# Score maxima in five rounds in place of six, with two more PSUM banks, in a gated cross-attention block

## The chip, the cores and the metric

One core of one Trainium2 chip runs the whole kernel. The metric is the device time in microseconds (us) of one execution. A core has five engines with instruction streams of their own: PE (TensorE, the matrix unit, whose weight loads are shown apart as PEld), DVE (VectorE), ACT (ScalarE), POOL (GpSimd) and SP (SyncE, which here issues all DMAs). They meet at semaphores alone. PSUM, where PE writes its results, has eight banks of 128 partitions x 512 fp32 numbers.

## The reference, cut to what matters

Four sequences of 2048 tokens of width 512 are attended, with 16 heads of width 32, to 154 context tokens each; a feed-forward part with a token shift follows. Both are gated and added to their input.

```
x = x + tanh(g_xattn) * xattn(layernorm(x), ctx, Wq, Wk, Wv, Wo)
x = x + tanh(g_ffn)   * ffn(layernorm(x), W_r, W_k, W_v, mu_r, mu_k)

xattn:  Q = q Wq^T, K = c Wk^T, V = c Wv^T            (16 heads of 32)
        out = softmax(Q K^T / sqrt(32)) V Wo^T
ffn:    xr, xk = mu * x + (1 - mu) * (x of the token before)
        out = sigmoid(xr W_r^T) * (square(relu(xk W_k^T)) W_v^T)
```

The change touches one step of the softmax alone: the largest score of each token and head, which is subtracted before the exponential. The values that are computed stay the same.

## The kernel before

**Tiling.** The 8192 tokens are cut into 16 blocks of 512. A block has four token tiles of 128 (t = 0 to 3), and the 16 heads are four groups (g = 0 to 3) of four heads (j = 0 to 3), where head j of a group lies on partitions 32j to 32j+31 (`rows(j)`). Each big product is made of high and low parts of its operands: 12 matmuls of 128x128 by 512 columns (`product`, L1075; `ffn_k` writes its own out, L1240).

**Software pipeline.** `step(i)` of each engine handles the attention of block i together with the feed-forward part of block i-1 and the queries of block i+1. Steps 1 to 14 are a hardware loop; step 0 computes the keys and values of the context in place of the feed-forward part, and step 15 has no next block. The order on every engine is written out by hand; nothing is planned at run time. A wait holds everything behind it on its engine.

**Banks.** `s_bank0` to `s_bank3` take scores, `o_bank` and `d_bank` take the attention's values and its denominators (and later transposed tiles and mixed inputs of the feed-forward part), `g_bank0` and `g_bank1` take the big products in turn.

**Score maxima.** For each of the 16 pairs (g, t), four matmuls, one for each head j, give 128 tokens x 154 scores (L1137); their weights and their moving rows lie on the 32 partitions of head j. Head j always writes `s_bank[j]`, where three pairs fit side by side. The pairs come in six *rounds* (`ROUNDS`, L183): rounds 0 to 2 are t = 0 to 2 of group r, round 3 is t = 3 of groups 0 to 2, round 4 is t = 0 to 2 of group 3, and round 5 is the pair (3, 3). After each round DVE takes four maxima with `reduce_max` (L854), one for each bank, over 462 columns (154 in round 5). PE starts a round when `reduced` says that DVE is through with the round before. When all are there, `maxima_transposed` (L1148) turns the maxima on PE into `o_bank`, ACT copies them to `mT`, and the scores of the exponential are made with them.

**Where the rounds lie in PE's order** (L1352 to L1374, then L1288 to L1295). In the second half of step i: `query(i+1, 0)`; `query(i+1, 1)` with round 0 ahead of its third chunk of three matmuls; `query(i+1, 2)` with round 1 ahead of its fourth; `project(i, 0)` (the attention's output product of token tile 0) with round 2 ahead of its fourth; `project(i, 1)`; `project(i, 2)` with round 3 ahead of its first; `x2_transposed(i, 0)` (the normalised tile, transposed); `project(i, 3)`; `x2_transposed(i, 1)`; `query(i+1, 3)` with `x2_transposed(i, 2)` in it; `x2_transposed(i, 3)`; `ffn_v(i-1, 3)`; round 4. Then in step i+1: `ffn_k(i, (0, 1))`; round 5; `ffn_k(i, (2,))`, two chunks, `maxima_transposed(i+1)`, two chunks.

**Who waits beside it.** `project(i, t)` for t of 2 and 3 waits for `residual` t-2 on DVE (`x1_ready`, L1206), because both use one g bank. `x2_transposed(i, 0)` waits for the chain residual 0 (L890), moments (L819 to L824) on DVE, three small operations on POOL (L441 to L447), and the normalisation on ACT (L600). DVE's own order in that stretch is (L1023 to L1050): `attend(i, 3)`, the maxima of rounds 0, 1 and 2, residual 0, two maxima of round 3, residual 1, the other two maxima of round 3, residuals 2 and 3, the last normalisation (L898), then the mixing of the feed-forward inputs (L908, L921, L788), which PE's `ffn_k` needs. In step i+1 it goes on with the maxima of round 4, `mix_r(i, 0)` (L931), and the maxima of round 5.

Of the kernel before, what the change touches and what calls it, by code (L numbers as in the profile page):

```python
# [13 lines left out]
HI, LO = 0, 1  # L14
# [3 lines left out]
def flamingo_block(nc, x, ctx_columns, g_xattn, g_ffn, Wq, Wk, Wv, Wo, W_r, W_k, W_v, mu_r, mu_k, out):  # L18
# [10 lines left out]
    G = H // 4  # L29
    N = 512  # L30
    TT = N // P
    BLOCKS = B * T // N
    PER_BATCH = T // N
    S = 154
    TAIL = 32
# [13 lines left out]
    with ExitStack() as ctx:  # L49
# [28 lines left out]
        buf4 = sb("buf4", [P, 2, C, N], F32R)  # L78
# [76 lines left out]
        max_done = sem("max_done")  # L155
# [26 lines left out]

        ROUNDS = [[(g, t) for t in range(3)] for g in range(3)] + [[(g, 3) for g in range(3)], [(3, t) for t in range(3)], [(3, 3)]]  # L183
        MAX_UNITS = 4 * len(ROUNDS)
        xT_bank = [d_bank, s_bank[1], s_bank[2], s_bank[3]]
# [33 lines left out]
        LATER_STORES = [16 * (B - 1) if kind == "k" else 16 for _, kind, _ in KV[G + 2:]]  # L219
        kv_bank = s_bank[0:3] + s_bank[0:1] + [o_bank, d_bank] + [g_bank[n % 2] for n in range(7)]  # L220

# [25 lines left out]
        def later(eng, semaphore, value):  # L247

            if not isinstance(value, int) or value > 0:
                eng.wait_ge(semaphore, value)  # L250
# [535 lines left out]
        def _(dve):  # L786
# [56 lines left out]

            def reduce_max(i, r, heads=range(4)):

                (g, t), pairs = ROUNDS[r][0], len(ROUNDS[r])
                for j in heads:
                    if r == j == 0:
                        later(dve, mT_done, i)
                    dve.wait_ge(max_done, i * MAX_UNITS + 4 * r + j + 1)  # L850
                    scores = s_bank[j][:, 0:S * pairs].rearrange("p (n s) -> p n s", n=pairs)
                    column = TAIL * j + g
                    maxima = mm[:, t:t + pairs, column] if ROUNDS[r][-1][1] > t else mm[:, t, column:column + pairs]
                    nc.vector.reduce_max(maxima, scores, AX.X).then_inc(reduced, 1)  # L854
# [97 lines left out]
            dve.wait_ge(small_loaded, 64)  # L952
            for r in range(4):
                reduce_max(0, r)
                if r < 3:
                    weight_low(range(2 * C + 2 * r, 2 * C + 2 * r + 2))
# [8 lines left out]
            def step(i, ffn, pre):  # L965
                reduce_max(i, 4)
                if ffn:
                    mix_r(i - 1, 0)
                else:
                    kv_low_part(G + 1)  # L970
                reduce_max(i, 5)
                if not ffn:
# [55 lines left out]
                residual(i, 0, pre)  # L1028
                if pre:
                    reduce_max(i + 1, 3, (0, 1))  # L1030
                residual(i, 1, pre)
                if pre:
                    reduce_max(i + 1, 3, (2, 3))
                residual(i, 2, pre)
# [39 lines left out]
        def _(pe):  # L1074
# [14 lines left out]
            def cols(n):  # L1089
                return slice(P * n, P * n + P)  # L1090

            def rows(j):
                return slice(DH * j, DH * j + DH)

            def keys_or_values(u):

                item, kind, n = KV[u]
                if u == 0:
                    pe.wait_ge(ctx_lo, TILES[0])
                elif u == 3:  # L1100
                    pe.wait_ge(kv_lo, 1)
                elif u == G:
                    pe.wait_ge(w_lo, 3 * C)
                elif u == FIRST_LATER:
                    pe.wait_ge(ctx_lo, TILES[0] + TILES[1])
                    pe.wait_ge(q_copied, G)
                elif u > FIRST_LATER + 1:
                    pe.wait_ge(kv_lo, u - 1)
                if kind == "k":
                    product(kv_product(u), lambda s, c: buf1[:, s, c, cols(n)], lambda m, c: ctx_parts[item][:, m, c, 0:P * TILES[item]], C,  # L1110
                            (lambda c: pe.wait_ge(w_lo, c + 1)) if u == 0 else None).then_inc(kv_done, 1)
                else:
                    product(kv_product(u), lambda s, c: ctx_parts[item][:, s, c, cols(n)], lambda m, c: buf2[:, m, c, :], C).then_inc(kv_done, 1)
# [12 lines left out]
            def maxima(i, r):  # L1126

                if r == 0:
                    pe.wait_ge(k_loaded, 16 * K_LOADS * (i + 1))
                    later(pe, p_lo, i * SCORE_UNITS)  # L1130
                    pe.wait_ge(xT_lo, (i + 1) * TT)
                else:
                    pe.wait_ge(reduced, i * MAX_UNITS + 4 * r)
                pe.wait_ge(q_hi, i * G + ROUNDS[r][-1][0] + 1)
                for n, (g, t) in enumerate(ROUNDS[r]):
                    for j in range(4):
                        ins = nc.tensor.matmul(s_bank[j][:, S * n:S * n + S], buf4[rows(j), HI, g, cols(t)], k_all[rows(j), g, :],  # L1137
                                               start=True, stop=True)
                        if n == len(ROUNDS[r]) - 1:
                            ins.then_inc(max_done, 1)  # L1140

# [72 lines left out]

            def x2_transposed(i, t):
                if t < TT - 1:
                    pe.wait_ge(xn2_ready, i * (TT - 1) + t + 1)
                else:
                    pe.wait_ge(xn2_last, i + 1)
                if t < 2:  # L1220
                    pe.wait_ge(attn32_ready, (i + 1) * G)
                else:
                    pe.wait_ge(x2_ready, i * TT + t - 1)
                transposed(x2_bank[t], [xn2[t % 2][:, cols(c)] for c in range(C)]).then_inc(x2_done, 1)
# [45 lines left out]
            def at(chunk, what):  # L1270
                return lambda c: what() if c == chunk else None
# [9 lines left out]
            query(0, 2, False, at(1, lambda: maxima(0, 1)))  # L1281
            query(0, 3, False, at(1, lambda: maxima(0, 2)))
            maxima(0, 3)
            keys_or_values(G)
            maxima(0, 4)

            def step(i, ffn, pre):
                if ffn:  # L1288
                    ffn_k(i - 1, (0, 1))
                    maxima(i, 5)  # L1290
                    ffn_k(i - 1, (2,), before=at(2, lambda: maxima_transposed(i)))
                else:
                    keys_or_values(G + 1)
                    maxima(i, 5)
                    maxima_transposed(i)  # L1295
# [56 lines left out]
                if pre:  # L1352
# [10 lines left out]
                    project(i, 1, pre)  # L1363
                    project(i, 2, pre, at(0, lambda: maxima(i + 1, 3)))
                    x2_transposed(i, 0)
# [6 lines left out]
                    if ffn:  # L1372
                        ffn_v(i - 1, 3)
                    maxima(i + 1, 4)  # L1374
                else:
                    ffn_r(i - 1, 3)
                    for t in range(3):
                        project(i, t, pre)
                    x2_transposed(i, 0)
                    project(i, 3, pre)  # L1380
                    x2_transposed(i, 1)
                    v_product(i - 1, 3, V3_END, lambda c: x2_transposed(i, c) if c >= 2 else None)

# [46 lines left out]
```

## Time and profile before

| | us |
|---|---|
| runs of the kernel before | 1411.4 median, 1409.05 to 1411.85 (3 runs) |
| the profiled execution's own time | 1411.68 |
| its span, first to last instruction | 1409.9 |
| PE busy | 1357.0 (96%) |
| DVE busy | 1043.5 (74%) |
| ACT busy | 777.4 (55%) |
| POOL busy | 574.7 (41%) |

The span is the time between the first and the last instruction; 1.8 us lie around it. A busy share is an average over stages, and matmuls are pipelined, so that a busy PE is not PE at its peak: small gaps between matmuls of different shape hide in it. The granted clock of PE was 0.989 of full speed over the span, and 1.00 in the steady blocks. In the timeline a row gives the start, the time from the first start to the last end, the engine, the line, the tiles and shapes, the number of instructions, and in brackets the idle time of the engine before it with what ended it.

### The profile page before, as it was taken

The numbers are of one execution on the slowest core, as the hardware profiler recorded it, in microseconds if no ns is written. First come the engines' busy times: TensorE is split into PE (matmuls) and PEld (weight loads), VectorE is DVE, ScalarE is ACT, GpSimd is POOL, SyncE is SP. The second block draws the span as 40 slices with busy tenths as digits, with TensorE's granted clock in tenths as the row PEclk, the third lists the DMA queues.
The fourth block names the chain that finished last, engine by engine and source line by source line (L and its number), as shares of the span: only waits on it lengthen the run. The fifth ranks groups of instructions, "written<-read, shape, count | busy, mean of one in ns | idle before, by whom it ended". The sixth has DMA issues, their size and how long they took to land.

```text
span 1409.9 us, 27976 instructions
## 1 busy us (share of the span) xinstructions
PE 1357.0 (96%) x9436; PEld 991.6 (70%) x9436; DVE 1043.5 (74%) x1940; ACT 777.4 (55%) x1440; POOL 574.7 (41%) x774
## 2 busy tenths in 40 slices
PE   4979999999999999999999999999999999999988
PEld 4657677776767777676777767677776767767667
DVE  4787868687786867778686876868777686877662
ACT  3583746647374663736456374655637465563632
POOL 2113535344352534435353353525344353444433
PEclk7999999999999999999999999999999999999999
DMA  6630121211112121111212011121202112110101
GB/s 187 218 93 18 53 61 52 74 51 42 33 60 67 52 73 37 46 44 60 67 52 66 24 66 44 60 67 52 60 22 74 44 52 74 52 57 17 46 23 46
DMA packets 98795, 84.07 MB, mean 60 GB/s; under 512 B 49488, under 2 KB 63824, under 8 KB 98768
## 3 DMA queue, kind: packets, MB, share of 16 engines
q1 hardware_dynamic: 98768, 83.72, 19.5%
q8 instruction: 15, 0.25, 0.1%
q14 instruction: 12, 0.10, 0.0%
HBM read 58.79 MB, written 20.71 MB: 56 GB/s over the span
## 4 chain that ended last, share of the span: by engine, by line
PE 79%; DVE 9%; ACT 8%; issue 3%; POOL 0%; DMA 0%; ACTq 0%; DVEq 0%
PE g_bank L1080 45%; PE g_bank L1240 7%; PE o_bank L1187 6%; PE s_bank L1161 4%; PE d_bank L1193 4%; ACT s_bank L641 3%; ACT pq L640 3%; PE s_bank L1137 3%; PE s_bank L1171 2%; DVE buf L788 2%; PE d_bank L1086 2%; DVE o_bank L921 2%; PE o_bank L1086 1%; DVE d_bank L921 1%; ACT buf L546 1%
## 5 line engine op out<-in xcount | busy, mean ns | idle before, releaser
L858 DVE TENSOR_TENSOR pq<-s_bank,pq 128x512 f16<-128x512 f32 x320 | 220.2, 689 | 70.2 <-ACT s_bank L641 70.0
L854 DVE TENSOR_REDUCE mm<-s_bank 128x3 f32<-128x462 f32 (+1 forms) x384 | 199.0, 579 | 93.2 <-PE s_bank L1137 93.0
L640 ACT ACTIVATE pq<-s_bank 128x512 f16<-128x512 f32 x320 | 192.3, 601 | 87.2 <-PE s_bank L1165 87.2
L1080 PE MATMUL g_bank<-xnT,WqT 128*128 128x512 f32 x768 | 200.0, 407 | 4.4 <-DVE xnT L842 4.4
L1240 PE MATMUL g_bank<-buf,WkT 128*128 128x512 f32 x744 | 195.8, 410 | 8.6 <-DVE buf L788 6.5
L641 ACT ACTIVATE s_bank<-s_bank 128x512 f32<-128x512 f32 x320 | 194.6, 608 | 0.0
L1080 PE MATMUL g_bank<-WoT,buf 128*128 128x512 f32 x768 | 193.3, 401 | 0.0
L1080 PE MATMUL g_bank<-WrT,buf 128*128 128x512 f32 x744 | 183.5, 395 | 0.0
L477 POOL TENSOR_TENSOR buf<-place,buf 128x512 fp32r<-128x512 f32 x64 | 82.5, 1290 | 235.9 <-ACT buf L546 235.9
L1080 PE MATMUL g_bank<-WvT,buf 128*128 128x512 f32 x708 | 174.2, 395 | 0.0
L1240 PEld LDWEIGHTS g_bank<-buf,WkT 128*128 128x128 f32 x744 | 136.0, 191 | 51.4 <-DVE buf L788 13.8
L1080 PEld LDWEIGHTS g_bank<-xnT,WqT 128*128 128x128 f32 x768 | 140.3, 191 | 40.7 <-DVE xnT L842 5.9
L1080 PEld LDWEIGHTS g_bank<-WrT,buf 128*128 128x128 f32 x744 | 137.3, 188 | 39.6 <-issue 10.9
L1080 PEld LDWEIGHTS g_bank<-WoT,buf 128*128 128x128 f32 x768 | 140.7, 188 | 32.7
L1080 PEld LDWEIGHTS g_bank<-WvT,buf 128*128 128x128 f32 x708 | 130.6, 188 | 32.6 <-issue 5.8
L465 POOL TENSOR_TENSOR buf<-xa,buf 128x512 fp32r<-128x512 f32 x64 | 82.1, 1283 | 161.9 <-DVE d_bank L921 82.0
L546 ACT ACTIVATE buf<-place 128x512 fp32r<-128x512 f32 x128 | 81.1, 633 | 107.0 <-DVE place L875 72.5
L473 POOL TENSOR_TENSOR buf<-place,buf 128x512 fp32r<-128x512 f32 x64 | 83.3, 1301 | 93.8 <-ACT buf L546 93.8
L485 POOL TENSOR_TENSOR x<-place,x 128x512 f32<-128x512 f32 x48 | 61.7, 1284 | 123.1 <-DVE place L885 123.1
L600 ACT ACTIVATE xa<-x,nb,rstd 128x512 f32<-128x512 f32 x48 | 39.0, 813 | 105.1 <-POOL nb L447 104.9
L469 POOL TENSOR_TENSOR place<-place 128x512 f32<-128x512 f32 x64 | 78.2, 1222 | 24.4 <-ACT place L632 24.4
L869 DVE STREAM_TRANSPOSE place<-d_bank 128x512 f32<-128x512 f32 x64 | 45.4, 709 | 55.5 <-PE d_bank L1193 55.5
(142 smaller groups left out, 2071.8 us busy)
## 6 DMA issues: line engine op xcount, KB each, us to landing
xa<-in_x SPq DMA_DIRECT2D x64, 256.0 KB, 3.4
x<-in_x SPq DMA_DIRECT2D x64, 256.0 KB, 2.7
out<-x SPq DMA_DIRECT2D x48, 256.0 KB, 2.0
k_all<-k_scratch SPq DMA_DIRECT2D x16, 256.0 KB, 2.8
k_low<-k_scratch SPq DMA_DIRECT2D x16, 256.0 KB, 3.0
v_main<-v_scratch SPq DMA_DIRECT2D x16, 256.0 KB, 2.8
place<-x SPq DMA_DIRECT2D x16, 256.0 KB, 2.4
out<-place SPq DMA_DIRECT2D x16, 256.0 KB, 2.0
```

The lines of the kernel that those rows point to most:

```text
L465: nc.gpsimd.tensor_tensor(buf4[:, LO, g, :], q32[g], buf4[:, HI, g, :].bitcast(F32), ALU.subtract).then_inc(q_lo, 1)
L469: nc.gpsimd.tensor_tensor(k2[c % 2], k2[c % 2], k2[c % 2], ALU.mult).then_inc(k2_ready, 1)
L473: nc.gpsimd.tensor_tensor(buf1[:, LO, c, :], k2[c % 2], buf1[:, HI, c, :].bitcast(F32), ALU.subtract).then_inc(k2_lo, 1)
L477: nc.gpsimd.tensor_tensor(buf3[:, LO, g, :], attn32, buf3[:, HI, g, :].bitcast(F32), ALU.subtract).then_inc(attn_lo, 1)
L546: nc.scalar.activation(dst, src, ACT.Copy).then_inc(done, 1)
L640: nc.scalar.activation(pq[:, n, HI, :], bank[:, :], ACT.Exp, scale=SCALE).then_inc(p_hi, 1)
L641: nc.scalar.activation(bank[:, :], bank[:, :], ACT.Exp, scale=SCALE).then_inc(p_full, 1)
L854: nc.vector.reduce_max(maxima, scores, AX.X).then_inc(reduced, 1)
L858: nc.vector.tensor_tensor(pq[:, n, LO, :], score_bank[5 * g + n][:, :], pq[:, n, HI, :], ALU.subtract).then_inc(p_lo, 1)
L1080: ins = nc.tensor.matmul(dst, stationary(s, c), moving(m, c), start=(c, n) == (0, 0), stop=(c, n) == (chunks - 1, len(PRODUCTS) - 1))
L1187: nc.tensor.matmul(o_bank[rows(j), :], v, pq[:, 4 if n else j, q, :], start=(n, k) == (0, 0), stop=(n, k) == (1, 2))
L1240: ins = nc.tensor.matmul(bank[c][:, :], WkT2[:, s, e, cols(c)], buf3[:, m, e, :], start=(e, n) == (0, 0), stop=(e, n) == (C - 1, len(PRODU ...
```

## The change

The rounds become lists of *units*: a unit is a bank, a head and the pairs (g, t) whose scores stand side by side in that bank, and one maximum on DVE. There are five rounds. Rounds 0 to 2 keep t = 0 to 2 of group r for all four heads in the s banks, and have two units more in `o_bank` and `d_bank`: in round 0 the pair (0, 3) of heads 0 and 1; in round 1 the pairs (0, 3) and (1, 3) of heads 2 and 3; in round 2 the pairs (1, 3) and (2, 3) of heads 0 and 1. The new round 3 is the former round 4. The new round 4 (the last) has the pair (3, 3) of heads 0 and 1, and (2, 3) and (3, 3) of heads 2 and 3. The 64 matmuls of a block are in rounds of 14, 16, 16, 12 and 6; the maxima are 6, 6, 6, 4 and 4 (26 where there were 24), over 154 columns four times, 308 six times and 462 sixteen times. Within a round the matmuls go pair by pair, and in each through the units in the order o, d, s0, s1, s2, s3.

The round ahead of `project(i, 2)` goes, and on DVE the two halves of its maxima between the residuals. Round 0 also waits for the attention of the block (`attn32_ready`), and `x2_transposed` of tiles 0 and 1 waits for all maxima of rounds 0 to 2 where it waited for the attention. In block 0 the context's value product `keys_or_values(G)` is placed ahead of the new round 3, and it and all later context products use the g banks, with waits for the queries' copies in place of the o and d banks.

```diff
@@ -180,8 +180,21 @@
-        ROUNDS = [[(g, t) for t in range(3)] for g in range(3)] + [[(g, 3) for g in range(3)], [(3, t) for t in range(3)], [(3, 3)]]
-        MAX_UNITS = 4 * len(ROUNDS)
+        def unit(bank, head, *pairs):
+            return bank, head, pairs
+        def alone(g):
+            return [unit(s_bank[j], j, *((g, t) for t in range(3))) for j in range(4)]
+        ROUNDS = [
+            [unit(o_bank, 0, (0, 3)), unit(d_bank, 1, (0, 3))] + alone(0),
+            [unit(o_bank, 2, (0, 3), (1, 3)), unit(d_bank, 3, (0, 3), (1, 3))] + alone(1),
+            [unit(o_bank, 0, (1, 3), (2, 3)), unit(d_bank, 1, (1, 3), (2, 3))] + alone(2),
+            alone(3),
+            [unit(s_bank[j], j, (3, 3)) for j in range(2)] + [unit(s_bank[j], j, (2, 3), (3, 3)) for j in (2, 3)]]
+        FIRST_UNIT = [sum(len(units) for units in ROUNDS[:r]) for r in range(len(ROUNDS) + 1)]
+        MAX_UNITS = FIRST_UNIT[-1]
         xT_bank = [d_bank, s_bank[1], s_bank[2], s_bank[3]]
@@ -217,7 +230,7 @@
         LATER_STORES = [16 * (B - 1) if kind == "k" else 16 for _, kind, _ in KV[G + 2:]]
-        kv_bank = s_bank[0:3] + s_bank[0:1] + [o_bank, d_bank] + [g_bank[n % 2] for n in range(7)]
+        kv_bank = s_bank[0:3] + s_bank[0:1] + [g_bank[(n + 1) % 2] for n in range(9)]
@@ -841,16 +854,15 @@
-            def reduce_max(i, r, heads=range(4)):
-
-                (g, t), pairs = ROUNDS[r][0], len(ROUNDS[r])
-                for j in heads:
-                    if r == j == 0:
+            def reduce_max(i, r):
+                for n, (bank, j, pairs) in enumerate(ROUNDS[r]):
+                    if r == n == 0:
                         later(dve, mT_done, i)
-                    dve.wait_ge(max_done, i * MAX_UNITS + 4 * r + j + 1)
-                    scores = s_bank[j][:, 0:S * pairs].rearrange("p (n s) -> p n s", n=pairs)
-                    column = TAIL * j + g
-                    maxima = mm[:, t:t + pairs, column] if ROUNDS[r][-1][1] > t else mm[:, t, column:column + pairs]
+                    dve.wait_ge(max_done, i * MAX_UNITS + FIRST_UNIT[r] + n + 1)
+                    (g, t), column = pairs[0], TAIL * j + pairs[0][0]
+                    scores = bank[:, 0:S * len(pairs)].rearrange("p (n s) -> p n s", n=len(pairs))
+                    maxima = mm[:, t, column:column + len(pairs)] if t == TT - 1 else mm[:, t:t + len(pairs), column]
                     nc.vector.reduce_max(maxima, scores, AX.X).then_inc(reduced, 1)
@@ -950,7 +962,7 @@
             dve.wait_ge(small_loaded, 64)
-            for r in range(4):
+            for r in range(3):
                 reduce_max(0, r)
@@ -963,12 +975,12 @@
             def step(i, ffn, pre):
+                reduce_max(i, 3)
+                if ffn:
+                    mix_r(i - 1, 0)
+                else:
+                    kv_low_part(G + 1)
                 reduce_max(i, 4)
-                if ffn:
-                    mix_r(i - 1, 0)
-                else:
-                    kv_low_part(G + 1)
-                reduce_max(i, 5)
                 if not ffn:
@@ -1026,11 +1038,7 @@
                 residual(i, 0, pre)
-                if pre:
-                    reduce_max(i + 1, 3, (0, 1))
                 residual(i, 1, pre)
-                if pre:
-                    reduce_max(i + 1, 3, (2, 3))
                 residual(i, 2, pre)
@@ -1095,6 +1103,8 @@
                 item, kind, n = KV[u]
+                if u in (G, G + 1):
+                    pe.wait_ge(q_copied, u - 1)
                 if u == 0:
@@ -1103,8 +1113,7 @@
                     pe.wait_ge(ctx_lo, TILES[0] + TILES[1])
-                    pe.wait_ge(q_copied, G)
-                elif u > FIRST_LATER + 1:
+                if u >= FIRST_LATER:
                     pe.wait_ge(kv_lo, u - 1)
@@ -1128,16 +1137,19 @@
                     later(pe, p_lo, i * SCORE_UNITS)
+                    later(pe, attn32_ready, i * G)
                     pe.wait_ge(xT_lo, (i + 1) * TT)
                 else:
-                    pe.wait_ge(reduced, i * MAX_UNITS + 4 * r)
-                pe.wait_ge(q_hi, i * G + ROUNDS[r][-1][0] + 1)
-                for n, (g, t) in enumerate(ROUNDS[r]):
-                    for j in range(4):
-                        ins = nc.tensor.matmul(s_bank[j][:, S * n:S * n + S], buf4[rows(j), HI, g, cols(t)], k_all[rows(j), g, :],
-                                               start=True, stop=True)
-                        if n == len(ROUNDS[r]) - 1:
-                            ins.then_inc(max_done, 1)
+                    pe.wait_ge(reduced, i * MAX_UNITS + FIRST_UNIT[r])
+                pe.wait_ge(q_hi, i * G + min(r, G - 1) + 1)
+                for n in range(3):
+                    for bank, j, pairs in ROUNDS[r]:
+                        if n < len(pairs):
+                            g, t = pairs[n]
+                            ins = nc.tensor.matmul(bank[:, S * n:S * n + S], buf4[rows(j), HI, g, cols(t)], k_all[rows(j), g, :],
+                                                   start=True, stop=True)
+                            if n == len(pairs) - 1:
+                                ins.then_inc(max_done, 1)
@@ -1212,15 +1224,17 @@
-            def x2_transposed(i, t):
+            def x2_transposed(i, t, pre=True):
                 if t < TT - 1:
                     pe.wait_ge(xn2_last, i + 1)
-                if t < 2:
+                if t >= 2:
+                    pe.wait_ge(x2_ready, i * TT + t - 1)
+                elif pre:
+                    pe.wait_ge(reduced, (i + 1) * MAX_UNITS + FIRST_UNIT[3])
+                else:
                     pe.wait_ge(attn32_ready, (i + 1) * G)
-                else:
-                    pe.wait_ge(x2_ready, i * TT + t - 1)
                 transposed(x2_bank[t], [xn2[t % 2][:, cols(c)] for c in range(C)]).then_inc(x2_done, 1)
@@ -1280,18 +1294,17 @@
             query(0, 3, False, at(1, lambda: maxima(0, 2)))
+            keys_or_values(G)
             maxima(0, 3)
-            keys_or_values(G)
-            maxima(0, 4)
                     ffn_k(i - 1, (0, 1))
-                    maxima(i, 5)
+                    maxima(i, 4)
                     ffn_k(i - 1, (2,), before=at(2, lambda: maxima_transposed(i)))
                     keys_or_values(G + 1)
-                    maxima(i, 5)
+                    maxima(i, 4)
                     maxima_transposed(i)
@@ -1361,7 +1374,7 @@
                     project(i, 1, pre)
-                    project(i, 2, pre, at(0, lambda: maxima(i + 1, 3)))
+                    project(i, 2, pre)
                     x2_transposed(i, 0)
@@ -1371,15 +1384,15 @@
                         ffn_v(i - 1, 3)
-                    maxima(i + 1, 4)
+                    maxima(i + 1, 3)
                 else:
                         project(i, t, pre)
-                    x2_transposed(i, 0)
+                    x2_transposed(i, 0, pre)
                     project(i, 3, pre)
-                    x2_transposed(i, 1)
-                    v_product(i - 1, 3, V3_END, lambda c: x2_transposed(i, c) if c >= 2 else None)
+                    x2_transposed(i, 1, pre)
+                    v_product(i - 1, 3, V3_END, lambda c: x2_transposed(i, c, pre) if c >= 2 else None)
```

## Rows read from the trace of the kernel before

**Rows 1.** The page's chain of work that ended last, by engine.

```profile
PE 79%; DVE 9%; ACT 8%; issue 3%; POOL 0%; DMA 0%; ACTq 0%; DVEq 0%
```

**Rows 2.** Windows: length, busy time of each engine (instructions), clock, DMA share, GB/s.

```profile
608.68:691.62 82.94, 82.14 (x582) 59.84 (x581) 63.40 (x118) 46.99 (x87) 35.63 (x48) 1.00 0.18 54
```

**Rows 3.** Critical chain of one block, in order: start, length, what.

```profile
630.96 0.62 PE d_bank L1086 x4
...
638.17 3.05 PE g_bank L1240 x12
```

**Rows 4.** Timeline, PE: round 3 and the product behind it.

```profile
620.51 0.57 PE L1137 MATMUL s_bank<-k_all,buf 32*128 32x154 f32 x12
621.01 3.06 PE L1080 MATMUL g_bank<-WoT,buf 128*128 128x512 f32 x12
```

**Rows 5.** Timeline, PE, single matmuls about round 3 and project(i, 2).

```profile
620.19 0.40 PE L1080 MATMUL g_bank<-WoT,buf 128*128 128x512 f32 x1
...
621.36 0.39 PE L1080 MATMUL g_bank<-WoT,buf 128*128 128x512 f32 x1
...
623.68 0.39 PE L1080 MATMUL g_bank<-WoT,buf 128*128 128x512 f32 x1
...
624.58 0.40 PE L1080 MATMUL g_bank<-WoT,buf 128*128 128x512 f32 x1
```

**Rows 6.** The same about round 5 and, last, behind `maxima_transposed`.

```profile
640.83 0.39 PE L1240 MATMUL g_bank<-buf,WkT 128*128 128x512 f32 x1
...
641.15 0.34 PE L1137 MATMUL s_bank<-k_all,buf 32*128 32x154 f32 x4
...
641.76 0.39 PE L1240 MATMUL g_bank<-buf,WkT 128*128 128x512 f32 x1
...
643.60 0.39 PE L1240 MATMUL g_bank<-buf,WkT 128*128 128x512 f32 x1
```

**Rows 7.** Three narrow stretches in round 2: matmuls running; the second holds two passes.

```profile
616.33 0.35 PE L1137 MATMUL s_bank<-k_all,buf 32*128 32x154 f32 x4
...
616.51 0.39 PE L1137 MATMUL s_bank<-k_all,buf 32*128 32x154 f32 x8
...
616.62 0.28 PE L1137 MATMUL s_bank<-k_all,buf 32*128 32x154 f32 x4
```

**Rows 8.** Timeline, DVE: maxima of rounds 1 and 2, residual 0.

```profile
613.43 2.28 DVE L854 TENSOR_REDUCE mm<-s_bank 128x3 f32<-128x462 f32 x4 [1.87 <-PE s_bank L1137]
...
616.92 2.28 DVE L854 TENSOR_REDUCE mm<-s_bank 128x3 f32<-128x462 f32 x4 [1.22 <-PE s_bank L1137]
619.12 0.68 DVE L890 TENSOR_TENSOR x<-g_bank,x 128x512 f32<-128x512 f32 x1
```

**Rows 9.** Timeline, DVE: maxima of round 5 and the next operation.

```profile
641.61 0.99 DVE L854 TENSOR_REDUCE mm<-s_bank 128x1 f32<-128x154 f32 x4
642.51 0.69 DVE L788 TENSOR_TENSOR buf<-d_bank,buf 128x512 fp32r<-128x512 f32 x1
```

**Rows 10.** Timeline: the normalisation of tile 0 on ACT, its transposes' weight loads on PE.

```profile
622.06 0.82 ACT L600 ACTIVATE xa<-x,nb,rstd 128x512 f32<-128x512 f32 x1 [6.64 <-POOL nb L447]
...
623.68 0.59 PEld L1086 LDWEIGHTS o_bank<-ident,xa 128*128 128x128 f32 x4
```

**Rows 11.** Timeline: `maxima_transposed`, weight loads on PE.

```profile
642.73 0.57 PEld L1086 LDWEIGHTS o_bank<-ident,mm 128*128 128x128 f32 x4
```

**Rows 12.** Timeline: DVE releases `x2_transposed(i, 3)`; the second matmul behind it.

```profile
630.30 0.55 DVE L898 TENSOR_SCALAR xa<-x,mv,rstd 128x512 f32<-128x512 f32 x1 [1.14 <-POOL rstd L443]
...
630.90 0.42 PEld L1086 LDWEIGHTS d_bank<-ident,xa 128*128 128x128 f32 x4 [0.38 <-DVE xa L898]
...
631.63 0.39 PE L1080 MATMUL g_bank<-WvT,buf 128*128 128x512 f32 x1
```

**Rows 13.** Timeline, block 0: the last maxima on DVE, their transposes on PE.

```profile
55.88 0.98 DVE L854 TENSOR_REDUCE mm<-s_bank 128x1 f32<-128x154 f32 x4
...
56.92 0.66 PE L1086 MATMUL o_bank<-ident,mm 128*128 128x128 f32 x4 [1.72 <-DVE mm L854]
```

More of the change, by code:

```diff
@@ L965, in step @@
             def step(i, ffn, pre):
-                reduce_max(i, 4)
+                reduce_max(i, 3)
                 if ffn:
@@ L970, in step @@
                     kv_low_part(G + 1)
-                reduce_max(i, 5)
+                reduce_max(i, 4)
                 if not ffn:
```

## The prediction

> **What bounds the kernel now.** I read the page's chain of waits first: PE is 79% of it, DVE 9%, ACT 8% [rows 1]. Then the windows: a steady block takes 82.94 us, in which PE is busy 82.14 us and DVE 63.40 [rows 2]. So PE has no room; whatever a round costs PE is paid in the block's time, as is whatever makes PE wait. But the chain leaves PE once in each block: from the end of `x2_transposed(i, 3)` at 631.58 (630.96 + 0.62) it runs over ACT and DVE and comes back to PE at 638.17 [rows 3]. That stretch hangs on `project(i, 3)` by residual 3, the last normalisation and the last transposes, so it starts later or earlier as `project(i, 3)` does, and PE's work beside it hides nothing. I therefore follow two things: when `project(i, 3)` runs, and when `maxima_transposed` runs. All behind each shifts with it.
>
> **What a round costs PE.** Round 3 has 12 matmuls; 0.50 us pass from its first to the next product's first [rows 4]. That is not all, since the weight loads are no longer ahead. From the last full matmul before it to the second behind it are 621.36 - 620.19 = 1.17 us; without the round two pitches would lie there, each (623.68 - 621.36) / 10 = 0.23 us [rows 5]. Cost: 0.71 us. For round 5 (4 matmuls) the same sum is 641.76 - 640.83 - 0.46 = 0.47 us [rows 6]. In round 2 the matmuls start in passes of four heads: 616.33, 616.51, 616.62 [rows 7]. So a further pass costs 0.11 us (0.12 by the difference of the two rounds), and a round has a fixed cost of about 0.36 us.
>
> Removing the round ahead of `project(i, 2)` gives back 0.71 us. Its scores come back elsewhere. What that costs depends on why four start together. If it is because they lie on different partitions, the passes of a round are as many as the matmuls of its commonest head. In the new round 0 heads 0 and 1 occur four times, in round 1 heads 2 and 3 five times, in round 2 heads 0 and 1 five times, in the last round heads 2 and 3 twice. That is 1, 2, 2 and 1 passes more: 0.11, 0.22, 0.22 and 0.11 us. If only the number of matmuls counts, they cost (0.71 - 0.47) / 8 = 0.03 us each: 0.06, 0.12, 0.12 and 0.06. From below zero is the bound (the matmuls hide between others); from above 0.18 us a pass, the longest distance in rows 7. I take the passes, since the trace shows starts in clusters with gaps between, not evenly. PE alone then gains 0.71 - 0.66 = 0.05 us a block: the change removes a fixed cost and pays nearly all of it in passes.
>
> The Trainium skill bears on this from two sides. "TensorE: Matmul & The Clock Gate", Part 3 (Packing small matmuls), says that a weight load overlaps running matmuls only where its row group is another one; by that, the repeated heads make passes. "TensorEngine Tiling (Array Packing)", Instruction Overhead, gives each matmul an overhead of about 60 cycles; by that the count matters, and the second sum holds. No row of before shows a head repeated out of turn.
>
> **What the maxima cost DVE.** Four maxima over 462 columns take 619.12 - 616.92 = 2.20 us, 0.55 each [rows 8]; over 154 columns 642.51 - 641.61 = 0.90 us, 0.225 each [rows 9]. Between them, 308 columns cost 0.39 us. Round 0 grows by 0.45 us, rounds 1 and 2 by 0.78 each, the last by 2 x 0.165 = 0.33; the two halves between the residuals (2.2 us) go. DVE idled 1.87 us before round 1's maxima and 1.22 us before round 2's [rows 8], so 0.45 and 0.78 are hidden. (Close: round 1's end now at 613.43 + 2.28 + 0.11 + 0.78 = 616.60, and PE wants round 2 at 616.33 + 0.33 = 616.66.) Round 2's 0.78 us are not hidden, for residual 0 stands right behind them.
>
> **First place: `x2_transposed(i, 0)`.** Residual 0 starts later by 0.33 us (passes of rounds 0 and 1) and 0.78: 619.12 + 1.11 = 620.23 us. In round 2 the first unit is complete at the third pass, as the first bank was before, so nothing is won there. Behind residual 0 come moments, POOL and ACT, all of which waited for their input: the normalisation ended at 622.06 + 0.82 = 622.88 us [rows 10], and ends now at 623.99. A release takes about 0.05 us (630.30 + 0.55 to 630.90 [rows 12]), so the transposes start at 624.04. PE wanted them at 623.68 [rows 10]; with 0.71 off and 0.55 on, at 623.52. (`project(i, 2)` itself needs residual 0: done at 620.91, released at 620.96, where PE could have begun its loads just before; 0.1 us, which drowns in the wait that follows.) So the slack of 0.75 us which these transposes had is overdrawn by 0.4 us. Behind released transposes the second matmul of the next product starts 631.63 - 630.90 = 0.73 us after [rows 12]: at 624.77, where it was at 624.58 [rows 5]. `project(i, 3)` is 0.19 us later, in place of 0.16 earlier. What was gained by residuals 1 and 2 being free of maxima helps nobody, as they wait for the projections or had time.
>
> **Second place: `maxima_transposed`.** DVE runs without a gap into the last round's maxima, so their end moves from 642.60 (641.61 + 0.99) to 642.93 [rows 9], release 642.98. PE wanted to load at 642.73 [rows 11], now 642.84 with the pass. The second matmul behind was at 643.60 [rows 6]; by the 0.73 it is now at 643.71, and if the 0.14 us of wait added to the pass in full, at 643.85. I take 0.13 us of loss. The new waits beside these cost nothing: for `attn32_ready` PE has 18 query matmuls, 4.2 us by the pitch, between the attention's last matmul and round 0, in which DVE needs four operations, each no longer than the 0.7 us of a 512-column one; and the maxima that `x2_transposed(i, 0)` waits for stand ahead of residual 0 on DVE. PE has queued behind `maxima_transposed` half of `ffn_k(2)` and the scores, for which ACT's exponentials wait, so the loss goes on.
>
> **Block 0.** The value product moved ahead of the round saves a stall, but kv_low_part and the later maxima wait for the same context product as before; I count nothing, with half a us to each side. The last maxima add their 0.33 us in full, since PE already waits 1.72 us for them [rows 13].
>
> **Sum.** `project(i, 3)` with a next block occurs in 15 blocks: 15 x 0.19 = 2.9 us. The last round outside block 0 occurs 15 times: 15 x 0.13 = 1.9. Block 0: 0.3. Together +5.1 us. The profiled execution took 1411.68 us (span 1409.9 and 1.8 around it), so 1416.8; the median of the runs is 0.3 us less: 1416.5 us.
>
> **The rivals.**
> *The count of matmuls decides.* Then residual 0 is 0.18 + 0.78 later, the second matmul of `project(i, 3)` is at 624.62, +0.04 us, and `maxima_transposed` costs 0.11, since there DVE decides. 15 x 0.15 + 0.3 = +2.6 us: 1414.0. If the added matmuls cost nothing at all, -0.14 and +0.11: 15 x -0.03 + 0.3 = -0.1 us, 1411.2. For it: four matmuls issue within hundredths. Against: the gaps of rows 7.
> *PE's saving is kept (the other side).* If the chain from round 2's maxima to `x2_transposed(i, 0)` is not what PE meets, as the slack of 0.75 us might be taken to mean, and the count decides, PE gains 0.71 - 0.30 = 0.41 us there and loses 0.06 to 0.11 in the last round: 15 x -0.33 + 0.3 = -4.7 us: 1406.7. It decides as soon as the normalisation of tile 0 ends before 623.2. Against it is plain adding: 0.78 us of maxima lie on that chain whatever PE does. A maximum over 308 columns would have to take under half of what I interpolate, or stand in DVE's idle time before the round ends.
> *A pass out of turn costs 0.18 us.* Residual 0 is then 0.54 + 0.78 later, `project(i, 3)` +0.40, the last round +0.20: 15 x 0.6 + 0.4 = +9.4 us: 1420.8.
>
> **How the numbers follow.** Forecast 0.50; count decides, or something near it, 0.27; dear passes 0.12; saving kept 0.11. This kernel's measurement can tell a change of 0.2%, 2.8 us, from none: 1408.6 to 1414.2. The forecast and the dear passes are slower (0.62), the count is within (0.27), the saving is faster (0.11). The range leaves out the saving and the worst of the dear passes: 1411.0 to 1420.0. The forecast's own range is 1414.5 to 1418.
>
> **What would show it.** Right: a steady block of 83.2 to 83.3 us; round 1 and 2 in five clusters of starts; residual 0 about 1.1 us later after round 2's start of before; in front of `x2_transposed(i, 0)` an idle PE weight path released by ACT L600, which rows 10 do not have; `maxima_transposed` released by DVE L854. Wrong: `x2_transposed(i, 0)` without a wait, or starts of repeated heads 0.03 us apart. A block under 82.7 us would refute the whole.

## The result, and the profile after

| | before | changed |
|---|---|---|
| median of the runs, us | 1411.74 (8 runs) | 1415.66 (8 runs) |
| ratio, 95% interval | | 1.0033 (1.0019 to 1.0046) |
| profiled execution, us (span) | 1411.68 (1409.9) | 1413.76 (1412.0) |
| a steady block, us | 82.94 [rows 2] | 83.34 |
| PE's granted clock over the span | 0.989 | 0.991 |

The change makes the kernel slower by 3.9 us at the median (0.28%; the ratio says 0.33%); the forecast was 1416.5 us and a block of 83.2 to 83.3. The two profiled executions differ by only 2.1 us, which misleads: the 14 blocks of the loop, cut at the same query matmul in both kernels, cost 5.7 us more (1167.74 - 1162.02), and what lies outside of them 3.6 less. A reader has to cut the span before comparing. Windows: length, busy time of each engine, clock, DMA share, GB/s; the changed kernel's start, its 14 blocks, one block, and last a stretch where its start differs.

```profile
0.00:103.05 103.05, 73.22 (x544) 54.77 (x545) 73.28 (x141) 61.98 (x116) 23.52 (x54) 0.90 0.54 169
103.05:1270.79 1167.74, 1152.83 (x8113) 837.60 (x8109) 888.85 (x1679) 656.37 (x1218) 496.73 (x657) 1.00 0.18 53
...
604.08:687.42 83.34, 82.45 (x585) 59.89 (x581) 63.52 (x120) 46.88 (x87) 35.61 (x47) 1.00 0.18 53
...
100.00:110.00 10.00, 9.72 (x85) 6.76 (x85) 7.06 (x14) 3.44 (x7) 2.52 (x2) 1.00 0.51 104
```

The same of the kernel before:

```profile
0.00:105.82 105.82, 76.95 (x544) 56.36 (x544) 72.16 (x139) 61.79 (x116) 22.80 (x54) 0.89 0.53 166
105.82:1267.84 1162.02, 1148.34 (x8112) 836.54 (x8108) 887.15 (x1651) 657.91 (x1218) 497.25 (x657) 1.00 0.18 53
...
100.00:110.00 10.00, 9.32 (x66) 5.46 (x66) 5.55 (x9) 4.17 (x9) 0.83 (x1) 0.83 0.41 85
```

And of a second execution of the changed kernel, under its own windows:

```profile
0.00:105.86 105.86, 76.96 (x544) 56.72 (x545) 73.11 (x141) 61.80 (x116) 23.52 (x54) 0.89 0.53 166
100.00:110.00 10.00, 9.27 (x66) 5.48 (x66) 5.55 (x9) 4.19 (x9) 0.79 (x1) 0.83 0.40 82
```

In one execution of the changed kernel the start took 103.05 us, in the other 105.86; a clock of 1.00 in one and 0.83 in the other between 100 and 110 us goes with it (these windows do not hold the same work, so the clock is a companion here, not a cause that was shown). So 2.8 us of the start come and go with one kernel, and are no part of the change. The steady blocks hardly vary: behind the first one they took 82.93 to 82.94 us before, 83.32 to 83.35 in the changed kernel, and 83.29 to 83.33 in its second execution, so differences under some 0.03 us between two kernels say nothing.

Within a block the changed kernel shows what was forecast. Timeline, round 2 to `project(i, 3)`; the block starts at 604.08, that of before at 604.36:

```profile
616.33 0.33 PE L1149 MATMUL o_bank<-k_all,buf 32*128 32x154 f32 x1
...
616.92 0.48 DVE L866 TENSOR_REDUCE mm<-o_bank 128x2 f32<-128x308 f32 x1 [0.65 <-PE s_bank L1149]
...
617.32 0.47 DVE L866 TENSOR_REDUCE mm<-d_bank 128x2 f32<-128x308 f32 x1
617.70 2.27 DVE L866 TENSOR_REDUCE mm<-s_bank 128x3 f32<-128x462 f32 x4
619.89 0.68 DVE L902 TENSOR_TENSOR x<-g_bank,x 128x512 f32<-128x512 f32 x1
...
620.62 2.62 PEld L1088 LDWEIGHTS g_bank<-WoT,buf 128*128 128x128 f32 x12 [0.25 <-DVE x L902]
...
622.84 0.81 ACT L613 ACTIVATE xa<-x,nb,rstd 128x512 f32<-128x512 f32 x1 [7.42 <-POOL nb L460]
...
623.77 0.42 PEld L1094 LDWEIGHTS o_bank<-ident,xa 128*128 128x128 f32 x4 [0.53 <-issue]
...
624.16 0.99 PEld L1088 LDWEIGHTS g_bank<-WoT,buf 128*128 128x128 f32 x5
```

Counted from the block's start, residual 0 begins at 15.81 us (before: 619.12 - 604.36 = 14.76), the normalisation of tile 0 ends at 19.57 (18.52), its transposes load at 19.69 (19.32 [rows 10]) behind an idle weight path of 0.53 us, and the next product's loads begin at 20.08 (624.24 - 604.36 = 19.88 before): 0.2 us late. The idle time is marked "issue", not ACT; that ACT is what PE waits for is read from the ACT row, which ends 0.12 us ahead, and put to the test by the second run below. At the second place:

```profile
641.09 0.46 PE L1149 MATMUL s_bank<-k_all,buf 32*128 32x154 f32 x6
641.48 1.65 PE L1254 MATMUL g_bank<-buf,WkT 128*128 128x512 f32 x6
641.53 1.31 DVE L866 TENSOR_REDUCE mm<-s_bank 128x1 f32<-128x154 f32 x4
642.97 0.42 PEld L1094 LDWEIGHTS o_bank<-ident,mm 128*128 128x128 f32 x4 [0.27 <-issue]
...
643.36 0.30 PEld L1254 LDWEIGHTS g_bank<-buf,WkT 128*128 128x128 f32 x2
```

The last round takes 0.39 us where it took 0.27, and the weight path, which showed no idle time before these transposes [rows 11], idles 0.27, again marked "issue". The waits of the whole trace, in which L1094 into `o_bank` stands for both places (total, times, longest), name ACT in two cases only:

```profile
PEld o_bank L1094 <- issue: 11.0, 28, 0.5
...
PEld o_bank L1094 <- ACT xa L613: 1.0, 2, 0.5
```

### The profile page after: what moved, and what is told of

Same layout as the page of the kernel before. It is cut to its first block, busy times and chain, and to the rows that moved or that the text cites. A ratio compares the mean times of both kernels' runs of the same rounds, so it can differ in the third digit from the quotient of the medians.

```text
span 1412.0 us, 27993 instructions
## 1 busy us (share of the span) xinstructions
PE 1356.7 (96%) x9436; PEld 989.8 (70%) x9436; DVE 1047.1 (74%) x1972; ACT 776.0 (55%) x1440; POOL 575.2 (41%) x774
## 4 chain that ended last, share of the span: by engine, by line
PE 79%; DVE 9%; ACT 8%; issue 3%; POOL 0%; DMA 0%; ACTq 0%; DVEq 0%
PE g_bank L1088 45%; PE g_bank L1254 7%; PE o_bank L1199 6%; PE s_bank L1173 4%; PE d_bank L1205 4%; ACT s_bank L654 3%; ACT pq L653 3%; PE s_bank L1183 2%; DVE buf L801 2%; PE o_bank L1094 2%; PE d_bank L1094 2%; PE s_bank L1149 2%; DVE o_bank L933 2%; DVE d_bank L933 1%; ACT buf L559 1%
## 5 line engine op out<-in xcount | busy, mean ns | idle before, releaser
L866 DVE TENSOR_REDUCE mm<-s_bank 128x3 f32<-128x462 f32 (+2 forms) x320 | 166.2, 583 | 1.3 <-PE s_bank L1149 1.3
L478 POOL TENSOR_TENSOR buf<-xa,buf 128x512 fp32r<-128x512 f32 x64 | 83.0, 1296 | 165.3 <-ACT xa L632 83.2
L486 POOL TENSOR_TENSOR buf<-place,buf 128x512 fp32r<-128x512 f32 x64 | 83.2, 1301 | 96.8 <-ACT buf L559 96.8
```

The source lines that it names most:

```text
L478: nc.gpsimd.tensor_tensor(buf4[:, LO, g, :], q32[g], buf4[:, HI, g, :].bitcast(F32), ALU.subtract).then_inc(q_lo, 1)
L486: nc.gpsimd.tensor_tensor(buf1[:, LO, c, :], k2[c % 2], buf1[:, HI, c, :].bitcast(F32), ALU.subtract).then_inc(k2_lo, 1)
```

## Experiments

All blocks below are windows of one steady block. Those with a ratio were run five rounds beside the kernel before; the others were executed once, and their times alone tell little.

**The changed kernel again.** No edit.

> The changed kernel unedited, as the base of the three beside it on the same chip. Theory (two waits: the transposes of tile 0 behind residual 0, and the transposed maxima behind the last round): a steady block of 83.34 us as in its first trace, where the kernel before has 82.94; 15 x 0.40 = 6 us, less what block 0 saves, so about 5 us (0.3 to 0.4%) slower than before. Rival (the difference is a clock effect of the start): a block of 83.34 us all the same, but a time within 0.2% of before.

```profile
608.08:691.37 83.29, 82.41 (x585) 59.91 (x581) 63.50 (x120) 46.86 (x87) 35.60 (x47) 1.00 0.18 53
```

1416.82 us against 1411.53, ratio 1.0041 (1.0025 to 1.0056). The slowdown is real.

**Round 2's o and d maxima behind residual 0.**

`reduce_max` takes the units to do as a third argument.

```diff
-                    reduce_max(i + 1, 2)
+                    reduce_max(i + 1, 2, range(2, 6))
                 residual(i, 0, pre)
+                if pre:
+                    reduce_max(i + 1, 2, (0, 1))
```

> The maxima over the o and d banks of round 2 are taken behind residual 0 and its moments, not ahead; nothing else is changed, and PE's order is the same. Theory: residual 0 comes 0.78 us earlier, the normalised tile 0 is there before PE wants it, the weight path has no idle time before the transposes of tile 0 that ACT ended, and project(i, 3) runs 0.19 us earlier than in the kernel before in place of 0.21 later. A steady block of 82.94 us, 0.40 less than the changed kernel, 15 x 0.40 = 6 us less in all. Rival (PE's added passes are the cost, the wait is incidental): the block stays at 83.3 us.

The block, and the first place (block start 603.45):

```profile
603.45:686.37 82.92, 82.11 (x584) 60.08 (x580) 63.51 (x120) 46.96 (x87) 35.62 (x47) 1.00 0.18 54
```

```profile
621.66 0.82 ACT L613 ACTIVATE xa<-x,nb,rstd 128x512 f32<-128x512 f32 x1 [6.87 <-POOL nb L460]
...
622.60 0.58 PEld L1098 LDWEIGHTS o_bank<-ident,xa 128*128 128x128 f32 x4
```

1411.35 us, ratio 1.0004 (0.9992 to 1.0017). The transposes load at 19.15 us of the block, 0.17 earlier than before and without a wait. One order on DVE is worth 0.4 us a block, as much as the whole loss. PE's order and its added passes were the same, so the rival falls. The block is that of before because two terms cancel: the 0.16 us that PE gains (0.71 less the passes of rounds 0 to 2) now show, and pay for the second place, whose loss is still there.

**The last round without its added pair.**

```diff
-            [unit(s_bank[j], j, (3, 3)) for j in range(2)] + [unit(s_bank[j], j, (2, 3), (3, 3)) for j in (2, 3)]]
+            [unit(s_bank[j], j, (3, 3)) for j in range(4)]]
```

> The pair (2, 3) of heads 2 and 3 is left out of the last round: its two matmuls and its columns in two maxima (four maxima over 154 columns remain, as in the kernel before), so those maxima are not computed. Theory: the transposed maxima are no longer late, 0.18 us less a block: 83.16 us, 2.7 us less in all. Rival (only PE's added pass counts there, DVE's 0.33 us are hidden): 0.11 us less, 83.23 us. Second rival (ACT's exponentials or DVE set the pace behind it and absorb the shift): no change, 83.34 us.

```profile
602.70:685.89 83.19, 82.30 (x582) 59.85 (x578) 63.18 (x120) 46.87 (x87) 35.66 (x47) 1.00 0.17 53
```

```profile
641.28 0.59 PEld L1094 LDWEIGHTS o_bank<-ident,mm 128*128 128x128 f32 x4
```

1412.2 us, ratio 1.0013 (1.0001 to 1.0024). The idle time of 0.27 us before the transposed maxima is gone, so it was DVE that PE waited for. But the block lies between the theory (83.16) and the pass alone (83.23) and does not tell them apart: it is 0.10 to 0.15 us under the two executions of the changed kernel, and the pass alone is 0.12. What the wait costs beside the pass is at most 0.06 us, and is not shown to be more than nothing. The second rival falls.

**Both at once.** The two edits above.

> The maxima over the o and d banks of round 2 behind residual 0, and the last round without the pair (2, 3) of heads 2 and 3 (its scores and maxima are left out). Theory (two losses that add, and under them PE's own saving): 83.34 - 0.40 - 0.16 = 82.78 us a block, 0.16 under the kernel before, some 2.4 us less than it in all, 0.17%. Rival (the two are one chain, of which one cure is enough): 82.94 us, as with the first cure alone.

```profile
602.25:685.05 82.80, 82.01 (x582) 60.03 (x578) 63.17 (x120) 46.98 (x87) 35.60 (x47) 1.00 0.18 54
```

1409.52 us against 1411.6, ratio 0.9985 (0.9976 to 0.9994). The two losses add (82.92 less 82.80 is 0.12, the pass again), so the rival of one chain falls. Rid of both, the five rounds are 0.14 us a block better than the six: what is left of the removed round's 0.71 us once the passes of rounds 0 to 2 are paid. But this kernel leaves one pair's maxima of two heads out, so it is no version to keep.

**The o and d matmuls of a round first.**

```diff
-                for n in range(3):
-                    for bank, j, pairs in ROUNDS[r]:
+                spare = len(ROUNDS[r]) - 4
+                for n, units in [(n, ROUNDS[r][:spare]) for n in range(2)] + [(n, ROUNDS[r][spare:]) for n in range(3)]:
+                    for bank, j, pairs in units:
```

> In rounds 0 to 2 PE does all matmuls of the o and d banks ahead of those of the s banks; the passes of a round stay as many. Theory: in round 2 the first maximum can start one pass, 0.11 us, earlier, and the whole chain over residual 0 to the transposes of tile 0 with it: a block of 83.23 us. Rival (the chain is not what binds): 83.34 us. If the passes are not set by the commonest head but by order, rounds 1 and 2 change their length of 0.71 us from first matmul to the next product's first.

```profile
603.16:686.37 83.21, 82.37 (x585) 59.95 (x581) 63.49 (x120) 46.88 (x87) 35.65 (x47) 1.00 0.18 53
```

1415.79 us, ratio 1.0031 (1.0019 to 1.0042). The block lost 0.13 us, as one pass earlier should give; the ratio alone could not have told it from the changed kernel. Round 2 kept its length: 0.72 us from its first matmul to the next product's (615.40 to 616.12), so the order of the matmuls within a round does not set it.

**What sets a round's length.** On the kernel before, repeated matmuls in rounds 0 and 1.

```diff
+                again = {0: [0, 1, 2, 3], 1: [0, 0]}.get(r, [])
                 for n, (g, t) in enumerate(ROUNDS[r]):
-                    for j in range(4):
+                    for k, j in enumerate((again if n == 2 else []) + [0, 1, 2, 3]):
...
-                        if n == len(ROUNDS[r]) - 1:
+                        if n == len(ROUNDS[r]) - 1 and k >= (len(again) if n == 2 else 0):
```

> A probe of what sets a round's length on PE, on the kernel before: round 0 repeats one pair for all four heads (16 matmuls, the commonest head four times), round 1 repeats it for head 0 alone, twice (14 matmuls, the commonest head five times), round 2 is left at 12. The repeated scores overwrite equal ones. Measured is the distance from a round's first matmul to the next product's first, 0.50 us for 12 in the kernel before. Theory (passes, as many as the matmuls of the commonest head, 0.11 us each): 0.61 us for round 0 and 0.72 for round 1. Rival (0.03 us for each matmul): 0.62 for round 0 and 0.56 for round 1.

Timeline, PE: 16 matmuls balanced over the heads, then 14 with one head five times, each with the product behind it.

```profile
608.69 0.68 PE L1138 MATMUL s_bank<-k_all,buf 32*128 32x154 f32 x16
609.29 3.69 PE L1080 MATMUL g_bank<-xnT,WqT 128*128 128x512 f32 x15
612.92 0.78 PE L1138 MATMUL s_bank<-k_all,buf 32*128 32x154 f32 x14
613.63 0.74 PE L1080 MATMUL g_bank<-xnT,WqT 128*128 128x512 f32 x2
```

0.60 us for 16 and 0.71 for 14: fewer matmuls, longer round. The commonest head counts, not the number. The rule that a weight load overlaps only with matmuls of other row groups (the Trainium skill, "TensorE: Matmul & The Clock Gate", Part 3) agrees; the sum by an overhead of each matmul falls. The kernel took 1416.28 us, its block 83.27, 0.33 more than before for 0.31 us of added passes: nothing hides a pass on PE.

```profile
604.37:687.64 83.27, 82.49 (x591) 60.16 (x587) 63.38 (x118) 46.98 (x87) 35.64 (x47) 1.00 0.18 53
```

**The slack in the kernel before.** Two, and then three, added maxima ahead of residual 0.

```diff
+                    if r == 2 and j == 3:
+                        for extra in range(2):
+                            nc.vector.reduce_max(mm[:, 0:2, 8 + extra], s_bank[j][:, 0:2 * S].rearrange("p (n s) -> p n s", n=2), AX.X)
```

> The kernel before, with two maxima over 308 columns added on DVE in round 2, ahead of its last one, into columns that nothing uses: 0.78 us more in front of residual 0 (what the change adds there), with PE's work as it was. Theory (the transposes of tile 0 had 0.75 us of slack and the chain adds one to one): they are released at about the moment at which PE wants them, a block of 82.94 to 82.97 us. Rival (the chain had no slack, all of it is lost): 83.7 us.

> The same with three added maxima, 1.17 us. Theory: the slack of 0.75 us is overdrawn by 0.42, of which the transposes give back 0.15 since their loads and matmuls are then closer: project(i, 3) 0.25 us later, a block of 83.19 us, and an idle time of PE's weight path before these transposes that ACT ended. Rival (more slack than 0.75 us): 82.94 us.

The blocks were 83.25 and 83.66 us. Both expectations miss, by 0.3 and 0.5 us. The single times were 1414.46 and 1425.01 us, where the kernel before took 1413.73: the second fits its block (11.3 us for 15 x 0.72), the first does not (0.7 us for 15 x 0.31), which a single execution cannot settle. The blocks and rows of the first and, below, of the second:

```profile
603.90:687.15 83.25, 82.22 (x585) 59.86 (x581) 64.06 (x120) 46.99 (x87) 35.63 (x47) 1.00 0.18 53
```

```profile
619.43 0.68 DVE L893 TENSOR_TENSOR x<-g_bank,x 128x512 f32<-128x512 f32 x1
...
620.35 0.57 PE L1140 MATMUL s_bank<-k_all,buf 32*128 32x154 f32 x12 [0.23 <-DVE x L893]
...
623.52 0.59 PEld L1089 LDWEIGHTS o_bank<-ident,xa 128*128 128x128 f32 x4
```

```profile
609.87:693.53 83.66, 82.26 (x585) 59.85 (x581) 64.42 (x121) 46.99 (x87) 35.62 (x47) 1.00 0.19 53
```

```profile
626.70 0.56 PE L1140 MATMUL s_bank<-k_all,buf 32*128 32x154 f32 x12 [0.61 <-DVE x L893]
```

In the kernel before, round 3 stands inside `project(i, 2)`, behind its wait for residual 0 (`x1_ready`, L1206). That gate shuts first: 0.78 us more cost 0.31, and 1.17 cost 0.72, so it had about 0.46 us of slack, and the round's fixed cost comes after it. The transposes behind had 0.75, but it was never they that PE met here: they loaded 0.3 us later than before (623.52 - 603.90 = 19.62 us of the block) and without a wait of their own. This is read from the rows; no run took the gate away. The change takes round 3 away from this gate, so that there the transposes decide; the prediction had both waits for the changed kernel, but my expectations for these two runs had forgotten the first.

**Block 0 in the old order.**

```diff
+            maxima(0, 3)
             keys_or_values(G)
-            maxima(0, 3)
```

and on DVE the maxima of round 3 of block 0 ahead of `kv_low_part(G)`.

> The changed kernel with the old order in block 0 alone: round 3 ahead of the context's value product, and its maxima ahead of kv_low_part(G). Theory (that move is what hid the 0.33 us that the last round's maxima grew by in block 0): from the first matmul of round 0 to the first of the transposed maxima 19.85 us in place of the 19.52 of both kernels. Rival (the g banks or their waits did it, or nothing had to be hidden): 19.52 us.

Rounds 0 and 3 and the transposed maxima on PE, and between them DVE and POOL:

```profile
37.32 0.30 PE L1150 MATMUL o_bank<-k_all,buf 32*128 32x154 f32 x1
...
48.87 0.57 PE L1150 MATMUL s_bank<-k_all,buf 32*128 32x154 f32 x12 [0.95 <-DVE mm L866]
...
57.87 0.66 PE L1095 MATMUL o_bank<-ident,mm 128*128 128x128 f32 x4 [2.25 <-DVE mm L866]
```

```profile
48.73 2.43 DVE L810 SCALAR_TENSOR_TENSOR WoT<-WoT_loaded,gate,WoT 128x512 fp32r<-128x512 f32 x2
```

```profile
49.12 1.50 POOL L478 TENSOR_TENSOR buf<-xa,buf 128x512 fp32r<-128x512 f32 x1 [2.12 <-ACT xa L632]
```

20.55 us (57.87 - 37.32), where both kernels have 19.52: the move hid 1.03 us, three times what was expected. What I had left out are the bigger maxima of rounds 0 to 2. With round 3 ahead of the value product PE waits 0.95 us for them, where it had no wait in the kernel before, and the value product behind it, for which ACT and then DVE wait, starts 12.05 us behind round 0 (49.37 - 37.32) in place of 10.64 before (48.04 - 37.40). The changed kernel has the product ahead of that wait.

**A try for a faster version.** The first edit, and `mix_r(0)` on DVE behind the last round's maxima, on ACT `mT_copy` ahead of `xr_high(0)`.

```diff
-                    mix_r(i - 1, 0)
...
                 reduce_max(i, 4)
+                if ffn:
+                    mix_r(i - 1, 0)
```

> Full computation. The maxima over the o and d banks of round 2 behind residual 0, and on DVE mix_r(0) behind the maxima of the last round, on ACT the copy of the transposed maxima ahead of the high part of that mix. Theory: the wait for DVE in front of the transposed maxima goes, which is the smaller half of the second loss (0.06 us; the other 0.12 is PE's added pass and stays): 82.88 us a block against 82.94 with the first edit alone, 0.9 us less. Rival: the mixed input comes 1.2 us later, and the feed-forward product that needs it, ffn_r(0), or the exponentials behind its high part on ACT wait: a block above 82.94 us.

1465.06 us, ratio 1.0380 (1.0365 to 1.0395): the rival, far beyond what I had given it. Two blocks, and the timeline around the exponentials:

```profile
621.85:708.68 86.83, 83.80 (x585) 60.97 (x581) 65.17 (x120) 47.11 (x87) 35.22 (x47) 0.98 0.17 51
708.68:794.50 85.82, 82.39 (x585) 60.03 (x581) 65.16 (x120) 47.11 (x87) 35.20 (x47) 1.00 0.17 52
```

```profile
662.12 0.69 DVE L802 TENSOR_TENSOR buf<-d_bank,buf 128x512 fp32r<-128x512 f32 x1 [1.28 <-ACT buf L559]
...
662.68 1.28 POOL L486 TENSOR_TENSOR buf<-place,buf 128x512 fp32r<-128x512 f32 x1 [3.08 <-ACT buf L559]
662.85 1.68 DVE L946 SCALAR_TENSOR_TENSOR d_bank<-place,mu,x 128x512 f32<-128x512 f32 x1
663.92 1.49 POOL L482 TENSOR_TENSOR place<-place 128x512 f32<-128x512 f32 x1
664.44 1.53 DVE L946 SCALAR_TENSOR_TENSOR o_bank<-place,mu,x 128x512 f32<-128x512 f32 x1
...
669.21 1.65 PE L1188 MATMUL s_bank<-buf,k_tail 128*128 128x512 f32 x3 [2.73 <-DVE pq L873]
```

```profile
669.00:671.20 2.20, 1.99 (x5) 1.61 (x6) 2.00 (x4) 2.20 (x6) 1.52 (x2) 0.50 0.00 0
```

The wait at the transposed maxima did go. But three things were lost. The moved mix came later, and DVE then idled 1.28 us for its high part from ACT: the low part above starts at 40.27 us of the block, with the first edit alone at 38.29 (641.74 - 603.45), 2.0 us earlier. Then two mixes, 0.76 us each with the first edit alone, ran beside POOL's operations and took 1.68 and 1.53 us, 1.7 more. ACT's high parts, its exponentials and the tail scores followed; PE idled 2.73 us, and in this block it then ran with a clock of 0.50, the lower of its two levels (1.2 GHz). In the next block the clock stayed at 1.00, and it took 85.82 us: so 2.9 us of the loss are the late chain, and about 1.0 more, in the blocks where the clock fell, is the clock. How the 2.9 divide between order and POOL was not tested. 0.06 us were to be had, about 3 to 4 were lost.

## Why the prediction was right

- **The path.** The steady block grew by 0.40 us (forecast 0.32), 0.38 of it at the two places named: with the first undone the block is that of before, with both 0.14 us under it. The signs given for the waits, weight loads released by ACT and by DVE, came as idle time marked "issue" nearly throughout; it is the two edits that show who was waited for.
- **Passes.** Forecast 0.11, 0.22, 0.22 and 0.11 us; rounds 0, 1, 2 and the last grew by 0.10, 0.21, 0.21 and 0.12. In round 2 the matmuls start in five clusters, at 616.34, 616.50, 616.62, 616.73 and 616.84, as forecast. The probe settles it against the count of matmuls.
- **Maxima.** Over 308 columns they start 0.40 us apart (616.92 to 617.32), interpolated were 0.39. Residual 0 was 1.05 us late, forecast 1.11.
- **First place.** 0.19 us forecast, 0.20 measured. Where nothing held the transposes, in the run with the maxima behind residual 0, they loaded at 19.15 us of the block; forecast were 623.52 - 604.36 = 19.16. The wait of `project(i, 2)` for residual 0 was 0.25 us, forecast 0.1, and did drown: what decides is the later of two waits on one chain.
- **Second place.** The term that was sized too small: 0.13 forecast, about 0.18 measured, 0.12 of it the pass and up to 0.06 the wait. I had let the released transposes win back nearly all of the wait, and the run without the pair leaves open whether they did.
- **Block 0.** Forecast 0.3 us of loss with half a us to each side; from round 0 to the transposed maxima there was none, 19.52 us in both. That the moved product would save as much as the maxima add I had not worked out; the run above gives 1.03 us, over a path that the forecast did not have.
- **The sum.** Forecast 5.1 us. By the traces it is 15 x 0.40 = 6.0 without the clock's share; the two comparisons gave 3.9 and 5.3 us, with intervals of 2.7 to 6.5 and 3.5 to 7.9 (the ratios' on 1411.6). The block was forecast 0.08 us too small, 1.2 us in all, and block 0 0.3 too large. Both 5.1 and 6.0 lie in both intervals, so the totals do not tell them apart, and that the median came within 0.9 us of the forecast is partly luck; what bears the forecast out is the block and the lengths of its rounds. Of the rivals, the count of matmuls (2.6 us) falls with the probe, the dear passes (9.4 us) with the passes of 0.10 to 0.12 us; the kept saving needed the first place to be free, and it took an edit to free it.

## What to carry to other kernels

Removing a stage from a loop gives back its fixed cost only if what it carried goes where nothing is waiting: here 0.71 us of PE came back, 0.64 were paid again in passes, and the maxima that moved stood ahead of the one operation whose chain PE needed next. Order work on a helper engine by who waits for it; two maxima that nothing waited for yet cost 0.4 us a block by standing first. And before moving an operation by a us on DVE, look at what POOL does at the new place, and list all gates on the chain, not only the one that is widest.

## What the runs showed of the hardware that I had not expected

A mix on DVE with inputs in SBUF took 1.68 and 1.53 us where POOL had started first, and 0.76 alone; two operations on a weight took 2.43 us beside POOL (49.12 + 1.50), and 1.41 in the kernel before, where POOL began only as they ended. "SBUF — State Buffer", Who interferes with whom, has this in the Trainium skill: DVE and GpSimd share a port pair, and a DVE instruction with two SBUF inputs contends with one of GpSimd that reads SBUF; the rows agree. They also show that the one that starts second pays: with the first edit alone a mix started 0.14 us ahead of POOL and kept its 0.76 us, while POOL's operation took 1.51, where the same one took 1.05 alone (start 649.69).

```profile
645.01 0.76 DVE L945 SCALAR_TENSOR_TENSOR d_bank<-place,mu,x 128x512 f32<-128x512 f32 x1
```

```profile
645.15 1.51 POOL L482 TENSOR_TENSOR place<-place 128x512 f32<-128x512 f32 x1
```

In a round of K = 32 matmuls the distance of the passes is 0.11 us whether a pass holds one matmul or four: 14 matmuls with one head five times took 0.71 us, 16 balanced ones 0.60.
